# A two-layer cross-attention kernel: layer 0's gates a slot later, layer 1's quantised rows half a slot to a slot later, and layer 1's bias added on VectorE

## The reference

```
x = x + xattn0(layernorm(x), ctx)     # 16 heads of 64: softmax(q k^T / 8) v, @ Wo + bo
x = x + ffn0(layernorm(x))            # (silu(x wg^T) * (x wu^T)) @ wd^T, hidden 768, integer weights / 127
x = x + xattn1(layernorm(x), ctx)     # as layer 0, other weights
x = x + ffn1(layernorm(x))            # rows quantised to -127..127 by their absolute maximum,
                                      # times a quantised 256x256 matrix, times both scales
```

## Time and profile before

| | |
|---|---|
| median of 3 runs | 1693.38 us (1689.7 to 1697.56) |
| profiled execution | 1690.04 us, span of its instructions 1688.0 us |
| busy share of the span | PE 93%, VectorE 81%, ACT 77%, POOL 73% |
| mean granted clock of PE | 0.973 of full |

### The profile page before, as it was taken

How to read it: one execution, slowest core, us unless ns; L and a number is a source line. 1 busy time by engine, 2 the same in 40 slices (tenths; PEclk the granted TensorE clock), 3 DMA queues, 4 the chain that set the end, 5 groups by cost and what they waited for, 6 DMA issues and landing times.

```text
span 1688.0 us, 75269 instructions
## 1 busy us (share of the span) xinstructions
PE 1568.0 (93%) x27538; PEld 1357.9 (80%) x27538; DVE 1364.3 (81%) x3490; ACT 1300.5 (77%) x5514; POOL 1232.4 (73%) x1966
## 2 busy tenths in 40 slices
PE   7999889999999999898999999999999999999995
PEld 4555578888888888888888889888888888888884
DVE  6777568787878778787878787788988988889886
ACT  6665678787877777787878777778888888888883
POOL 5120278787778787777877787778888888888884
PEclk9999999999999999999999999999999999999998
DMA  9998699867777777767676879879998888888995
GB/s 257 350 309 271 167 203 163 167 149 161 156 157 161 156 159 162 154 155 165 148 163 153 161 153 168 149 157 191 197 196 189 196 196 190 193 198 189 188 187 111
DMA packets 740023, 307.79 MB, mean 182 GB/s; under 512 B 629201, under 2 KB 725361, under 8 KB 737841
## 3 DMA queue, kind: packets, MB, share of 16 engines
q1 hardware_dynamic: 738049, 299.32, 81.1%
q0 software_dynamic: 1840, 6.82, 1.4%
HBM read 87.09 MB, written 65.54 MB: 90 GB/s over the span
## 4 chain that ended last, share of the span: by engine, by line
POOL 40%; issue 21%; PE 17%; DVE 5%; ACT 2%; DMA 2%; SPq 1%; POOLq 0%; DVEq 0%; ACTq 0%
POOL pr L1710 16%; PE psum L333 15%; POOL p L1723 11%; POOL p L1715 6%; POOL hT_l L1701 5%; POOL rs L395 2%; DMA pT<-p 2%; DVE sg L1515 2%; ACT th L1405 1%; DVE hf L1526 1%; PE psum L1278 1%; SPq L1129 1%; PE psum L1241 1%; DVE mv L384 1%; POOLq L274 0%
## 5 line engine op out<-in xcount | busy, mean ns | idle before, releaser
L1425 ACT ACTIVATE ex<-psum,nmax 128x77 f32<-128x77 f32 x2048 | 638.4, 340 | 21.2 <-DVE nmax L1550 15.1
L1425 ACT ACTIVATION_READ_ACCUMULATOR ex<-psum,nmax 128x1 f32 x2048 | 451.6, 221 | 0.0
L1715 POOL TENSOR_TENSOR p<-pr,p 128x308 f16<-128x308 f32 x512 | 386.9, 756 | 39.0 <-ACT p L348 0.6
L1710 POOL TENSOR_TENSOR pr<-ex,rden 128x308 f32<-128x308 f32 x512 | 373.8, 730 | 36.1 <-DVE rden L1555 36.0
L333 PE MATMUL psum<-xT,wq_h 128*64 128x256 f16 x4064 | 364.1, 281 | 0.0
L333 PE MATMUL psum<-xT,wq_l 128*64 128x256 f16 x2032 | 285.5, 277 | 0.0
L1550 DVE TENSOR_REDUCE nmax<-psum 128x4 f32<-128x308 f32 x512 | 238.1, 466 | 52.7 <-PE psum L1241 52.0
L1723 POOL CAST p<-pr 128x308 f16<-128x308 f32 x509 | 246.1, 483 | 40.8 <-DMA pT<-p 8.5
L333 PE MATMUL psum<-wo_h,oT_h 128*64 128x256 f16 x1792 | 251.4, 276 | 11.6 <-DVE oT_l L362 11.2
L333 PE MATMUL psum<-wo_l,oT_h 128*64 128x256 f16 x1792 | 250.0, 274 | 0.0
L333 PE MATMUL psum<-wo_h,oT_l 128*64 128x256 f16 x1792 | 250.0, 274 | 0.0
(11 more groups left out here) (172 smaller groups left out, 3604.1 us busy)
## 6 DMA issues: line engine op xcount, KB each, us to landing
keys<-ks SPq DMA_DIRECT2D x16, 1232.0 KB, 7.8
kb<-keys SPq DMA_DIRECT2D x256, 77.0 KB, 2.7
vb<-vals SPq DMA_DIRECT2D x128, 154.0 KB
vals<-vs SPq DMA_DIRECT2D x64, 256.0 KB, 4.2
x_pair<-in_x_dram SPq DMA_DIRECT2D x32, 256.0 KB, 3.0
pT<-p SPq DMA_TRANSPOSE x512, 3.3
x_res<-in_x_dram SPq DMA_DIRECT2D x32, 256.0 KB, 3.1
mid_x<-y SPq DMA_DIRECT2D x32, 256.0 KB, 2.6
```

The source lines that it names most:

```text
L1425: last = act.activation(ex[i][:, t, b, :], SC[:, t, b * NK:(b + 1) * NK], ACT.Exp, bias=nmax[i][:, t, b:b + 1], accum_out=den[i][:, t, b:b ...
L1710: pool.tensor_tensor(pr[:, t, :, :], ex[i][:, t, :, :], r, ALU.mult).then_inc(s_p, 1)
L1715: pool.tensor_tensor(d[:, t, 1, :, 0:NK], pr[:, t, :, :], d[:, t, 0, :, 0:NK], ALU.subtract).then_inc(s_pl, 1)
```

## The change

All arithmetic of layer 0 stays; what moves is where in the bodies it stands. Gates 0 and 1 go from slot 2 to slot 3, gates 2 and 3 from slot 3 to slot 0 of the next body, gates 4 and 5 from slot 0 to slot 1, with their ACT, VectorE and POOL parts. The steps that lead to them move too: spreads and moments of `x1` stay in slot 0 but come later in it, POOL's `rs` goes from slot 3 to slot 0 behind the half of unit 0, the normalisation to slot 1, the high part of `x216` to the end of slot 1, its low part and SP's transposition to slot 2, behind both transpositions of unit 1. `inverse` and `shift` of the first norm go to slot 2 on POOL.

In layer 1 the scale pair goes from slot 1 to slot 2, the rounding `q_i` from ahead to behind the queries' low half in slot 2, the turning, `qiT` and the product to slot 3, `ya` and `yo` to slot 0 of the next body, the store to its slot 1. The bias of layer 1, four matmuls with `pick` per body, leaves PE; VectorE adds it to `x_res` instead.

The core of the diff, cut:

```
@@ uses(lay): the order of the two shared banks
                 if u == 0 and lay[-3] == 0:
-                    out += [("gu", 4), ("gu", 5)]
+                    out += [("gu", 2), ("gu", 3)]
                 if u == 1:
+                    if lay[-3] == 0:
+                        out += [("gu", 4), ("gu", 5)]
...
                 if u == 3 and lay[-2] == 0:
-                    out += [("gu", 2), ("gu", 3)]
+                    out += [("gu", 0), ("gu", 1)]
...
@@ SP
-                        if u == 0 and lay[-3] == 1:
-                            store_output(h - 3 - B)
...
-                        if u == 1 and lay[-2] == 0:
-                            turn_second_rows(h - 2)
                         if turning:
                             turn_probabilities(n + u - 1, (u - 1) % UNITS, 1)
+                        if u == 2 and lay[-2] == 0:
+                            turn_second_rows(h - 2)
+                        if u == 1 and lay[-3] == 1:
+                            store_output(h - 3 - B)
...
@@ PE
-                        if u == 1 - l:
-                            product(pe, OA[:, t, :], pick, bo_rows[:, l, :], True, start=False, stop=False,
+                        if u == 1 and l == 0:
+                            product(pe, OA[:, t, :], pick, bo_rows[:, :], True, start=False, stop=False,
...
                         if u == 0 and lay[-3] == 0:
+                            gate_up(2, bank("gu", 2))
+                        if u == 1 and lay[-3] == 0:
                             gate_up(4, bank("gu", 4))
                         if lay[0] is not None:
                             scores(n + u, u, 32 * (h + 1))
                         if u == 3 and lay[-2] == 0:
-                            gate_up(2, bank("gu", 2))
...
+                            gate_up(0, bank("gu", 0))
...
@@ VectorE
+                    def scaled_rows(g, places):
+                        for t in range(QT):
+                            dve.wait_ge(s_a1, QT * g + t + 1)
+                            dve.scalar_tensor_tensor(out=ya[:, t, :], in0=RG[places["quant", t][0]][:, 0, :],
+                                                     scalar=lsc[:, t:t + 1], in1=rhs_sb[:, :], op0=ALU.mult,
+                                                     op1=ALU.mult).then_inc(s_ya, 1)
+
+                    def output_sum(g, residual):
+                        dve.wait_ge(s_ya, QT * (g + 1))
+                        after(dve, s_yo, 16 * g)
+                        dve.tensor_tensor(yo[:, :, :], ya[:, :, :], residual[:, :, :], ALU.add).then_inc(s_ysum, 1)
...
-                        if u == 0 and lay[-2] == 0:
-                            dve.wait_ge(s_x1, h - 1)
-                            spreads(dve, x1[1 - odd], st2, s_st2)
...
+                        if u == 0 and lay[-3] == 0:
+                            low_hidden(1, h - 3)
+                        if u == 0 and lay[-2] == 0:
+                            dve.wait_ge(s_x1, h - 1)
+                            spreads(dve, x1[1 - odd], st2, s_st2)
+                        if u == 0 and lay[-2] == 0:
+                            moments(dve, 1, st2, mv2, ve2, s_st2, s_mv2, h - 2)
+                        if u == 0 and lay[-3] == 0:
+                            sigmoid_gate(3, h - 3)
+                            hidden(3, h - 3)
+                        if u == 1 and lay[-2] == 0:
+                            normalise_rows(dve, 1, x2, x1[1 - odd], mv2, rs2, h - 1, s_x2)
...
+                        if u == 2 and lay[-1] == 1:
+                            dve.wait_ge(s_xr, 16 * h)
+                            bias = bo_b[:, 1, :].unsqueeze(1).to_broadcast([P, QT, D])
+                            dve.tensor_tensor(x_res[:, :, :], x_res[:, :, :], bias, ALU.add).then_inc(s_xb, 1)
...
+                        if u == 0 and lay[-3] == 1:
+                            scaled_rows(h - 3 - B, kinds[like - 1][1])
...
                         if lay[0] is not None and not (u == 2 and lay[-2] == 0):
                             reciprocals(n + u, u % 2, 0)
...
+                        if u == 0 and lay[-3] == 1:
+                            output_sum(h - 3 - B, x1[odd])
...
@@ POOL
                         if u == 0 and lay[-3] == 0:
+                            low_hidden(0, h - 3)
+                        if u == 1 and lay[-3] == 0:
                             low_hidden(2, h - 3)
+                        if u == 2 and lay[-3] == 0:
+                            low_hidden(5, h - 3)
...
-                        if u == 0 and lay[-3] == 0:
+                            probabilities(h + (u - 1) // UNITS, (u - 1) % UNITS, 1)
+                        if u == 1 and lay[-3] == 0:
                             low_hidden(3, h - 3)
...
+                        if u == 0 and (lay[-2] == 0 or lay[-3] == 0):
+                            inverse(pool, 1, ve2, rs2, h - 1)
```

More of the change, by code:

```diff
@@ L1092, in xattn_ffn_kernel @@
             assert all(kinds[h] == kinds[first] for h in range(first, last))
+        for h in range(B + 3, NB - 4):
+            assert all(kinds[h][1][use][0] == kinds[B + 3][1][use][0] for use in (("quant", 0), ("quant", 1)))
         def bodies(eng, body, steps=(2, 2)):
@@ L1459, in body @@
                             high(act, qT_h[(u + 1) % 2][:, :, :], RG[(u + 1) % 2], Q_DOWN).then_inc(s_qh, 1)
+                        if lay[0] is not None:
+                            exponentials(n + u, u % 2, 0)
                         if u == 2 and lay[-2] == 1 and like <= NB:
@@ L1568, in body @@
                             maxima(n + u, u % 2, 0)
-                        if u == 0 and lay[-2] == 0:
-                            moments(dve, 1, st2, mv2, ve2, s_st2, s_mv2, h - 2)
                         if lay[-1] is not None:
@@ L1602, in body @@
                             low_q(dve, (u + 1) % 2, RG[(u + 1) % 2]).then_inc(s_ql, 1)
+                        if u == 2 and lay[-2] == 1:
+                            dve.wait_ge(s_qa, QT * (h - 1 - B))
+                            after(dve, s_qt, h - 2 - B)
+                            dve.tensor_scalar(q_i[:, :, :], q_a[:, :, :], MAGIC + INT8_MAX, MAGIC,
+                                              ALU.min, ALU.subtract).then_inc(s_qi, 1)
+                        if u == 0 and lay[-3] == 0:
+                            low_hidden(1, h - 3)
[4 more added lines that the diff above has]
+                            moments(dve, 1, st2, mv2, ve2, s_st2, s_mv2, h - 2)
+                        if u == 0 and lay[-3] == 0:
+                            sigmoid_gate(3, h - 3)
+                            hidden(3, h - 3)
+                        if u == 1 and lay[-2] == 0:
+                            normalise_rows(dve, 1, x2, x1[1 - odd], mv2, rs2, h - 1, s_x2)
+                        if u == 1 and lay[-3] == 0:
+                            sigmoid_gate(5, h - 3)
+                            hidden(5, h - 3)
                         if u == 0 and lay[-2] == 1:
@@ L1673, in body @@
-                        if u == 3 and lay[-2] == 1:
-                            dve.wait_ge(s_ya, QT * (h - 1 - B))
-                            after(dve, s_yo, 16 * (h - 2 - B))
-                            dve.tensor_tensor(yo[:, :, :], ya[:, :, :], x1[1 - odd][:, :, :], ALU.add).then_inc(s_ysum, 1)
+                        if u == 0 and lay[-3] == 1:
+                            output_sum(h - 3 - B, x1[odd])
+                        if u == 3 and like == NB + 1:
+                            output_sum(h - 2 - B, x1[1 - odd])
@@ L1723, in probabilities @@
                         pool.tensor_copy(p16[v % 2][:, t, 0, :, 0:NK], pr[:, t, :, :]).then_inc(s_ph, 1)
-                        if between is not None:
-                            low_hidden(*between)
                         low_of(b, v, t)
@@ L1754, in body @@
                             shift(pool, 2, mv3, rs3, h - 2)
[L1755 to L1757 removed]
+                        if u == 3 and lay[-1] == 1 and lay[-2] == 1:
                             inverse(pool, 1, ve2, rs2, h)
```

199 lines of the change are left out of this document (78 added, 121 removed).

## The result

The changed kernel takes 1788.01 us (median of four runs, 1786.07 to 1790.81) where the kernel before takes 1695.47 (1689.7 to 1698.22): ratio 1.0552, 95% interval [1.0518, 1.0586]. The forecast was 1766, range 1722 to 1795, slower. The profiled executions have spans of 1788.8 and 1688.0 us.

What follows compares the result with a forecast made beforehand. PE was taken as nearly full with three engines close behind, so order decides. The profiled 1690.0 us plus 49 for layer 0 and 28 for layer 1 gave 1767, taken as 1766 us, range 1722 to 1795.

Steps and rivals of the forecast that it cites:

- VectorE's slot 0 and POOL's chain: Layer 0: VectorE's first reciprocal at S0 + 6.24 (S0: scores of slot 0 start) holds POOL; down 0 starts at S0 + 16.0.
- The sum without a fall of the clock: Layer 0 body at full clock: 16.0 until down 0 plus 11.24 to the next scores, 27.2 us against 26.35.
- The second path: Layer 0: SP issues x2's transposition later, it lands at S0 + 22.7 and holds gate 0; next scores at S0 + 28.7.
- The clock: Layer 0: a 3 us wait before down 0 lowers PE's clock in each body, 1.55 us more: 27.2 becomes 28.8.
- Rival (d): As the forecast, but each layer 0 body loses clock twice, another 0.8 us a body: 1790 us, 10 in 100.
- (a) to (c): Rivals, in us: even slots win 1587, layer 0 even 1714, layer 0 alone slows 1732; chances 7, 13, 15 in 100.
- The edges of layer 0: Layer 0's +49 us counted some 30 bodies at 1.64: 29 whole ones, the last three mixed ones as one.
- Layer 1: Layer 1's moved steps and bias add cost 0.95 us per body, +28 us over 29 bodies.
- 0.83 for ya and yo in slot 0: Layer 1: ya and yo in slot 0 make the first maximum of slot 1 start 0.83 us later, at 5.76.
- 0.35 for the turning and 0.15 for q_a against 0.37 for the scale pair: Layer 1, per body: turning in slot 3 costs 0.35 us, q_a 0.15; the scale pair leaving slot 1 gives back 0.37.
- The upper end of the range: The range's end of 1795 us, from 1.55 us lost twice in a body or from the blocked add.
- the blocked adds: Layer 1: each VectorE bias add caught behind a POOL instruction, 12 us more over the layer; left out of the sum.

Runs made afterwards that it cites:

- run 3: Changed kernel with VectorE's first reciprocal of layer 0's slot 0 moved right behind the low half of the queries: 1746.63 us, ratio 1.0345.
- runs 4 and 5: Changed kernel with VectorE's first reciprocals of slots 0 and 1 earlier: 1739.08 us; with SP's transposition of unit 3's second half also ahead of the x rows: 1690.63 us.
- Run 6: Changed kernel with SP's transposition of x2 issued ahead of that of unit 1's second half, nothing else: 1739.04 us, ratio 1.0287.
- run 8: Changed kernel with layer 1's last sum yo moved from slot 0 to slot 3, its store likewise: 1764.41 us, ratio 1.0429.
- run 11: Changed kernel with five order repairs (1622.36 us), then layer 1's bias back on PE and VectorE's add taken out: 1623.16 us, ratio 0.9606.

## Why the prediction was right, and which of its steps were not

**VectorE's slot 0 and POOL's chain.** Right: S0 + 5.91 for 6.24, the wait of hf of chunk 4 (1.45 for 1.7) and down 0 at S0 + 15.86 for 16.0. The price that was off is hT_l of chunk 1, 0.41 beside an idle POOL in place of 0.74. That the reciprocal is what holds the chain is shown by run 3, that the second one and SP's queue stand right behind it by runs 4 and 5.

**The sum without a fall of the clock.** 16.0 + 11.24 = 27.2. Run 6 shows this body: 27.20 us at a granted clock of 1.00, with down 0's wait unchanged.

**The second path.** Right: x2T sets gate 0 at S0 + 22.8 in nearly every steady body, and the next S0 follows 6.0 later, at S0 + 28.8 for 28.7 (down 0 to down 0, the same length, in the two bodies shown). I had set it beside the clock as a second way to the same number and concluded that a full clock would not help much; the 6 steady bodies at full clock show that, held at 28.8 by x2T alone.

**The clock, the step that failed.** I charged 1.55 us to each body, since a wait of 3 us in one piece should bring a fall every time, and about half the bodies had one before. Before, 16 of 24 steady bodies have a lowered clock, and now 18: it falls hardly more often than it did. The wait of 3 us alone doesn't bring it, for run 6 keeps the wait and has 6 such bodies. The price was right: in run 6 gate 0 starts 6.8 us after down 0 in a body with an ordinary fall and 5.2 in one without. So where the clock falls in the changed kernel, PE would be at gate 0 some 6.8 us after down 0, and x2T lets it start at 6.9: the two ways tie there, as forecast. By the falls alone my terms would give 27.2 + 18/24 x 1.55 = 28.4 us; the mean came out at 29.0 because x2T holds the other bodies at the same length, and 0.2 comes on top, from two long falls and a later down 0 in four bodies. That "each body" was wrong did not show in the total is luck. Rival (d), the clock lost twice in each body, has the nearest total (1790) and not the cause: two of 24 bodies are of its kind. (a) to (c) asked for an earlier down 0, for gate 0 in time or for slack in layer 1, and the rows show none of them.

Run 6 needs the same care. It takes away the wait for x2T and gains 1.26 us a body, but the clock also falls in 6 bodies there and not in 18. With run 6's lengths of a body (27.2 at full clock, 28.75 with an ordinary fall, 30.0 with a long one) and the changed kernel's 16 ordinary and 2 long falls, a body would take 28.5 us. By this estimate about 0.5 of the 1.26 is the wait for x2T and 0.7 the rarer falls, and why they became rarer no run shows.

**The edges of layer 0** were sized too small: between the first residual add and the end of the mixed bodies the change costs 67.3 us, for the 49 forecast. I took the last three bodies as one whole one. The last five cost 17.6 us more, where the 49 leave 3.1 for them (28 bodies before them at 1.64) and five full ones would be 8.2: the gates of slot 1 meet the turning of layer 1's rows in the two shared banks (6.2 us of waits for hf), and x2T comes up to 2.8 us late (8.7 us in four waits). Run 6 gives back 11.3 in the last five. The first four cost 9.6 in place of 6.6, half of it in the first of them. In the profiled execution, 1790.8 us, these 18 us and the 5.7 of the opening are nearly all of the 25 above 1766. I had not followed the mixed bodies one by one in the order.

**Layer 1.** +0.95 forecast, +0.95 measured, 26.4 us for 28. The first maximum of slot 1 starts at S0 + 5.94 (5.76 forecast), on VectorE's timeline of the body that starts at 1414.58, with POOL's and VectorE's rows for the bias add:

```profile
1419.50 1.00 DVE L1557 TENSOR_TENSOR yo<-ya,x 128x512 f32<-128x512 f32 x1
...
1420.52 0.44 DVE L1544 TENSOR_REDUCE nmax<-psum 128x4 f32<-128x308 f32 x1
...
1408.42 0.98 POOL L1718 TENSOR_TENSOR pr<-ex,rden 128x308 f32<-128x308 f32 x1
1409.46 0.79 POOL L1731 CAST p<-pr 128x308 f16<-128x308 f32 x1
...
1408.76 1.18 DVE L1668 TENSOR_TENSOR x_res<-x_res,bo_b 128x512 f32<-128x512 f32 x1
```

The step "0.83 for ya and yo in slot 0" fits run 8, where yo alone is worth 0.92. My 0.35 for the turning and 0.15 for q_a against 0.37 for the scale pair, 0.13 in sum, are not borne out: with yo out of the way they come to 0.04, the bias included. No run has one of them alone. Also mis-sized: yo and the add take longer than the 0.82 of the earlier trace rows, 1.0 and 1.2 us, both beside instructions of POOL; that this costs the body anything is not shown by a run.

The Trainium skill (SBUF — State Buffer, Summary: rules for kernel authors) says that of a VectorE instruction with two SBUF inputs and a GpSimd one that reads SBUF, the second to issue is blocked until the first has finished. I had left it out of the sum. The rows agree in part: the add takes 1.18 in place of 0.82, but POOL's pr, which started first, also takes 0.98 in place of 0.70, and its cast 0.79 in place of 0.44. The spans of pr and of the add overlap by 0.64 us, and no row shows which of the two stood still in that time. What it comes to in the body no run tells: taking the add off VectorE altogether (run 11) left layer 1's body as it was.

**The upper end of the range.** 1795 does not follow from the two terms named for it: 1.55 more in 30 bodies would be 1766 + 46 = 1812, the blocked adds 1766 + 12 = 1778. The measured 1788 lies 7 us under that end.

## What to carry to other kernels

When instructions are moved round a body in which several engines stand close to full, follow the engine that feeds the late consumer, and ask for each small instruction which everyone waits for (here a reciprocal of 0.17 us) what now stands ahead of it in its queue. Count DMA queues as engines: of the 95 us that the change cost, 49 went with one exchange of two issues on SP, a part of them by a clock that fell less often, and one sum in another slot of VectorE was worth 24 (21 by the ratios). A change that makes the kernel slower may still hold the better plan: in the new slots PE's body of layer 0 came down to 25.0 us, after 27.3, once the waits that the move had made were taken out one by one; behind the first reciprocal stood the second, then SP's order, then x2T.
